# First attention layer: scores formed a second time by key tile, in place of transposed probabilities

## The chip, the cores and the metric

The kernel runs on one core of one Trainium2 chip. The metric is the device time of one execution in microseconds. The engines are TensorE (matmuls and transposes, results to PSUM), VectorE, ScalarE and GpSimd, each with a queue of its own that it works off in order; semaphores tie them together.

## The reference

The program is two layers, each an attention and a feed-forward part, with layer norms ahead. Only the first attention is touched. For x of 8 batches x 512 tokens x 256 columns, with 16 heads of 16 columns:

```python
q = _lora(x, Wq, Aq, Bq)   # and k, v: x @ W.T + a low-rank term, 16 heads of 16
s = jnp.einsum('bhqd,bhkd->bhqk', q, k) / math.sqrt(DH)
alibi = slopes[:, None, None] * (i - j)
mask = jnp.triu(jnp.full((T, T), -jnp.inf), 1)
s = s + alibi[None] + mask
p = jax.nn.softmax(s, axis=-1)
o = jnp.einsum('bhqk,bhkd->bhqd', p, v)
return o @ Wp.T
```

The layer norm of x goes in, and the result is added to x.

## The kernel before, in words

The first attention is `attention0` (L767). It goes batch by batch: batches 0, 1 and 7 are written out, batches 2 to 6 are one hardware loop (`run`, `batch`). A batch has 48 slots; each engine issues for slot k the work of its own function `slot`, so the order on each engine is fixed by hand. For k below 47 the slot of the batch before, number k + 48, follows in the same place, which is how the end of one batch lies in the start of the next.

A head has three slots, 3h, 3h+1 and 3h+2, for the groups of query tiles (0, 1), (2) and (3); a query tile i of 128 rows needs keys 0 to (i+1)*128. The order of one group is:

- Stack. q and k are held as sums of bf16 parts, 96 rows (`TERMS0`) and 6 more for the position term, together `K0` = 102. They lie by token in `q_stage` and `k_stage`; TensorE transposes a head's eight tiles into a work bank (L950, kind "stack"), and ScalarE (even heads, L1060) or VectorE (odd heads, L1135) copies it to one of two places of `stack`: query columns 0 to 511, key columns 512 to 1023. It is filled three slots ahead.
- Scores (L901), by query tile: a bf16 product over the 102 rows, and for the tile's last 128 columns the mask added by a product with the identity (L902). The result lies in one of two score banks `S`. It waits until the exponential of the group two before is done (`s_exp`).
- `row_max` on VectorE (L1117): the negative maximum of each row to `neg_max`.
- `exp` on ScalarE (L1037), with the negative maximum as bias, one instruction for each query tile, to `prob` in fp32.
- `transpose_probs` on TensorE (L915), four slots behind (`LAG_T`): the head's ten 128 x 128 tiles to the three banks `PT`, by key tile.
- One slot later (`LAG_EV`) the copies to `probT`: 512 columns by ScalarE (L1045), 512 and 256 by VectorE (L1125).
- PV (L929) for four heads at once, in three parts at slots 17, 20, 23 and so on every 12: fp32, the key tiles of `probT` against 32 columns of values, the heads side by side in the array.

Beside it run the other jobs of a batch (`work`), which share the two work banks `W` in turn; a fill waits until the bank's content of two fills before is taken (`taken`). They are the transposes of normalized x for the next batch ("xT", L959, slots 24 to 33), the q and k pieces ("piece", L965), the values (L972), the transposes of a four-head output ("oT", L980; taken by a reciprocal L1159 and a product L1163 into `y`), of `y` ("yT", L986) and the output projection ("proj", L992; taken by L1172 into x with its statistics L1175). ScalarE takes in the same slot (`LAG_WA` = 0), VectorE one slot later (`LAG_WV` = 1). VectorE's order within a slot is: row maximum, normalization, the takes, the copies to `probT`. GpSimd forms the bf16 parts of the pieces; before the first batch it writes constant columns into the stages, and TensorE's first fill waits for that (`s_const`).

Of the kernel before, what the change touches and what calls it, by code (L numbers as in the profile page):

```python
# [14 lines left out]
P = 128  # L15
# [16 lines left out]
K0 = TERMS0 + 6  # L32
# [18 lines left out]
LAGS0 = (4, 1)  # L51
# [715 lines left out]
def attention0(block, x_sb, stats, consts, w, sem, sb, banks, lags, at):  # L767
# [3 lines left out]
    LAG_T, LAG_EV = lags  # L771
# [12 lines left out]
    IN_GROUP = {i: (g, sum((j + 1) * P for j in tiles if j < i)) for g, tiles in enumerate(GROUP_TILES) for i in tiles}  # L784
    S, PT, W, ob = banks[0:2], banks[2:5], banks[5:7], banks[7]
# [8 lines left out]
    prob = [sb(f"prob0_{g}", [P, 2, n], F32) for g, n in enumerate(GROUP_COLS)]  # L794
    probT = sb("probT0", [P, 2, 4, T_AT[3]], F32)
    one = sb("one0", [P, 1], F32)
    neg_max = sb("neg_max0", [P, QT], F32)
# [9 lines left out]
    s_exp = sem("probs_ready")  # L807
    s_pt = sem("probs_transposed")
    s_pta = sem("probsT_first_taken")
    s_ptv = sem("probsT_rest_taken")  # L810
# [19 lines left out]
    s_one = sem("one_ready")  # L830
# [58 lines left out]
    def _(pe):  # L889
        work_banks = Banks()  # L890

        def scores(b, h, g):
# [3 lines left out]
            wait(pe, s_exp, G - 1)  # L896
            off = 0
            for i in GROUP_TILES[g]:
                L = (i + 1) * P
                out = S[(3 * h + g) % 2][:, off:off + L]  # L900
                pe.matmul(out, stack[0:K0, h % 2, i * P:(i + 1) * P], stack[0:K0, h % 2, T:T + L], start=True, stop=False)  # L901
                last = pe.matmul(out[:, L - P:L], ident_b[:, :], mask[:, :], start=False, stop=True)  # L902
                off += L
            last.then_inc(s_scores, 1)

        def transpose_probs(b, h, r):
            H = b * HEADS + h
            if r == 0:
                wait(pe, s_exp, 3 * (H + 1))
                wait(pe, s_pta, H)  # L910
            else:
                wait(pe, s_ptv, 2 * H - 2 + r)
# [4 lines left out]
            last.then_inc(s_pt, 1)  # L917

        def pv(b, c, part):
            Q = b * QUADS + c  # L920
            if part == 0:
                wait(pe, s_oT, Q)
                wait(pe, s_pta, 4 * (Q + 1))
            else:
                wait(pe, s_ptv, 8 * Q + 6 + part)
# [77 lines left out]
        def prologue():  # L1003
            pe.wait_ge(s_const, 1)
# [6 lines left out]
        def slot(cur, off, k, last):  # L1011
# [3 lines left out]
            if 0 <= k - LAG_T < GROUPS:  # L1015
                transpose_probs(b, (k - LAG_T) // 3, (k - LAG_T) % 3)
# [10 lines left out]
    def _(act):  # L1027
        work_banks = Banks()

        def exp(b, h, g):  # L1030
            wait(act, s_max, b * GROUPS + 3 * h + g + 1)
            if g == 0:
                wait(act, s_pt, 3 * (b * HEADS + h - 1))
            off = 0
            for i in GROUP_TILES[g]:
                L = (i + 1) * P
                last = act.activation(prob[g][:, h % 2, off:off + L], S[(3 * h + g) % 2][:, off:off + L], ACT.Exp, bias=neg_max[:, i:i + 1])  # L1037
                off += L
            last.then_inc(s_exp, 1)

        def take_probs(b, h):
            H = b * HEADS + h
            wait(act, s_pt, 3 * H + 1)
            wait(act, s_pv, b * QUADS + h // 4 - 1)
            act.activation(probT[:, (h // 4) % 2, h % 4, T_AT[0]:T_AT[1]], PT[0][:, :], ACT.Copy).then_inc(s_pta, 1)  # L1045
# [7 lines left out]
        def take(kind, b, *a):  # L1053
            bank, n = work_banks.next(kind)
            if kind == "stack":
                h, = a
                if h % 2 == 0:
                    wait(act, s_st, b * HEADS + h + 1)
                    wait(act, s_scores, 3 * (b * HEADS + h - 1))
# [32 lines left out]
        def slot(cur, off, k, last):  # L1092
# [4 lines left out]
            if k < GROUPS:  # L1097
                exp(b, k // 3, k % 3)
# [1300 lines left out]
```

## Time and profile before

| what | value |
|---|---|
| median of 3 runs | 2374.68 us (2374.14 to 2378.23) |
| profiled execution, whole | 2372.82 us |
| its span, first to last instruction | 2371.0 us |
| mean granted TensorE clock | 0.941 |
| TensorE busy | 1977.4 us (83%), 18502 matmuls |
| VectorE busy | 1754.0 us (74%) |
| ScalarE busy | 1472.8 us (62%) |
| GpSimd busy | 1034.1 us (44%) |
| first score matmul of this attention | 60.7 us |
| end of this attention | about 646 us |

A busy share is that of the whole span. The ends of matmuls are modelled, since they are pipelined; starts are recorded, so the distance from one start to the next tells what a matmul costs when TensorE does not stand.

### The profile page before, as it was taken

To read this page: it belongs to the slowest core of one execution; us is meant where nothing else is said; L and a number is where in the kernel's file an instruction comes from. 1 tells how busy PE (TensorE), PEld (TensorE's weight loads), DVE (VectorE), ACT (ScalarE), POOL (GpSimd) and SP (SyncE) were. 2 spreads that over 40 slices of the span, in tenths; PEclk is the share of its full clock that TensorE was granted. 3 is DMA by queue.
4 is the path that set the end of the run, shared out by engine and by line. 5 is a ranking of instruction groups with operands and counts; after the bars stand their busy time and mean duration, and the time that the engine had idled before them with its cause. 6 is when DMAs were issued, how large, how long until landed. Compare 5 with 4: busy or idle time off the path is not lost. (4 is left out here: it accounts for less than half of the span.)

```text
span 2371.0 us, 56863 instructions
## 1 busy us (share of the span) xinstructions
PE 1977.4 (83%) x18502; PEld 1432.5 (60%) x18503; DVE 1754.0 (74%) x3653; ACT 1472.8 (62%) x2928; POOL 1034.1 (44%) x1226
## 2 busy tenths in 40 slices
PE   2889888899862997488798999989898999639999
PEld 1667666666561665155566766666766667526665
DVE  4788878778782443477687787869697887679997
ACT  1877767677662444186678686858687787434443
POOL 4434534245014000589656465657466563042222
PEclk8999999999956999799999999999999999869999
DMA  7000000000043332002100000000000000100000
GB/s 235 2 1 2 1 1 0 1 1 1 3 144 113 100 87 74 4 13 39 15 2 3 2 3 2 2 3 2 3 2 3 2 2 2 38 0 14 18 15 25
DMA packets 53144, 57.93 MB, mean 24 GB/s; under 512 B 7120, under 2 KB 47216, under 8 KB 52896
## 3 DMA queue, kind: packets, MB, share of 16 engines
q1 hardware_dynamic: 46240, 45.00, 6.1%
q0 software_dynamic: 6656, 9.85, 2.0%
q8 instruction: 128, 2.10, 0.4%
q14 instruction: 120, 0.98, 0.1%
HBM read 36.22 MB, written 18.61 MB: 23 GB/s over the span
## 5 line engine op out<-in xcount | busy, mean ns | idle before, releaser
L1037 ACT ACTIVATE prob_sb<-a_bank,neg_max_sb 128x128 f32<-128x128 f32 (+3 forms) x512 | 258.4, 530 | 133.8 <-DVE neg_max_sb L1117 122.1
L372 PE MATMUL a_bank<-w_in_sb,xnT_sb 128*128 128x512 f16 x1152 | 289.5, 389 | 30.7 <-DVE t_buf_sb L580 22.3
L1117 DVE TENSOR_REDUCE neg_max_sb<-a_bank 128x1 f32<-128x128 f32 (+3 forms) x512 | 237.5, 485 | 101.4 <-PE a_bank L902 87.8
L532 DVE TENSOR_REDUCE neg_max_sb<-a_bank 128x1 f32<-128x128 f32 (+3 forms) x512 | 235.7, 481 | 97.3 <-PE a_bank L289 96.6
L435 ACT ACTIVATE prob_sb<-a_bank,neg_max_sb 128x128 f32<-128x128 f32 (+3 forms) x512 | 259.7, 538 | 58.6 <-DVE neg_max_sb L532 55.9
L443 ACT ACTIVATE p_hi_sb<-a_bank 128x384 f16<-128x384 f32 (+1 forms) x384 | 204.9, 534 | 112.2 <-PE a_bank L298 111.1
L539 DVE TENSOR_TENSOR p_lo_sb<-a_bank,p_hi_sb 128x384 f16<-128x384 f32 (+1 forms) x384 | 227.5, 594 | 52.3 <-ACT p_hi_sb L443 49.8
L454 ACT ACTIVATE stack_sb<-a_bank 128x1024 f16<-128x1024 f16 (+1 forms) x256 | 210.1, 821 | 32.2 <-PE a_bank L343 30.5
L298 PE MATMUL a_bank<-ident_f_sb,prob_sb 128*128 128x128 f32 x1280 | 206.9, 276 | 0.6 <-ACT prob_sb L435 0.6
L915 PE MATMUL a_bank<-ident_f_sb,prob_sb 128*128 128x128 f32 x1280 | 205.9, 276 | 0.0
L708 POOL TENSOR_TENSOR rope_w_sb<-t_buf_sb,sin_sb 128x256 f32<-128x256 f32 x128 | 125.3, 979 | 169.6 <-DVE t_buf_sb L580 167.7
L318 PE MATMUL a_bank<-v_stage_sb,p_hi_sb 128*128 128x65 f16 x1280 | 159.2, 194 | 36.7 <-DVE y_sb L551 35.9
L372 PEld LDWEIGHTS a_bank<-w_in_sb,xnT_sb 128*128 128x128 f16 x1152 | 104.5, 100 | 138.4 <-DVE t_buf_sb L580 30.7
L284 PE MATMUL a_bank<-stack_sb 128*128 128x128 f16 (+3 forms) x512 | 149.4, 304 | 39.5 <-ACT prob_sb L435 29.3
L714 POOL TENSOR_TENSOR rope_z_sb<-rope_u_sb,rope_w_sb 128x512 f32<-128x512 f32 x128 | 162.4, 1269 | 24.0 <-POOL rope_w_sb L710 21.4
L1220 POOL TENSOR_TENSOR parts_sb<-rest_sb,one_sb 128x256 bf16<-128x256 f32 x64 | 39.2, 613 | 297.7 <-DVE rest_sb L1142 296.5
L580 DVE SCALAR_TENSOR_TENSOR t_buf_sb<-a_bank,bias_sb 128x512 f32<-128x512 f32 x192 | 131.5, 685 | 43.5 <-PE a_bank L372 31.0
L319 PE MATMUL a_bank<-v_stage_sb,p_hi_sb 128*128 128x65 f16 x1280 | 160.0, 197 | 0.0
L320 PE MATMUL a_bank<-v_stage_sb,p_lo_sb 128*128 128x65 f16 x1280 | 158.2, 193 | 0.0
L285 PE MATMUL a_bank<-stack_sb 128*128 128x128 f16 (+3 forms) x512 | 155.3, 303 | 0.0
L901 PE MATMUL a_bank<-stack_sb 102*128 102x128 bf16 (+3 forms) x512 | 143.0, 305 | 12.3 <-ACT prob_sb L1037 10.3
L587 DVE TENSOR_TENSOR rope_u_sb<-t_buf_sb,cos_sb 128x512 f32<-128x512 f32 x128 | 131.4, 1027 | 28.7 <-POOL rope_z_sb L714 16.3
(259 smaller groups left out, 5503.5 us busy)
## 6 DMA issues: line engine op xcount, KB each, us to landing
sorted_rows<-zeros_sb SPq DMA_DIRECT2D x1, 4992.0 KB, 22.4
x_in_sb<-sorted_rows SPq DMA_DIRECT2D x39, 128.0 KB, 2.1
sorted_results<-y_moe_sb SPq DMA_DIRECT2D x39, 128.0 KB, 1.7
x_sb_sb<-L_attn_x SPq DMA_DIRECT2D x8, 512.0 KB, 10.5
w_raw_sb<-L_ffn_gate_bank SPq DMA_DIRECT2D x8, 512.0 KB, 3.5
w_raw_sb<-L_ffn_up_bank SPq DMA_DIRECT2D x8, 512.0 KB, 4.4
w_raw_sb<-L_ffn_down_bank SPq DMA_DIRECT2D x8, 512.0 KB, 6.0
out<-x_sb_sb SPq DMA_DIRECT2D x32, 128.0 KB, 1.7
```

The costliest lines, as they stand in the source:

```text
L298: last = pe.transpose(PT[g][:, n * P:(n + 1) * P], prob[g][:, n * P:(n + 1) * P], ident_f[:, :])
L319: pe.matmul(o, hi, v[:, 65:130], start=False, stop=False)
L372: last = pe.matmul(out, xnT[:, x, c, j * P:(j + 1) * P], w["in"][:, w_, c, cols], start=k == 0, stop=k == len(terms) - 1)
L435: last = act.activation(prob[g][:, off:off + L], S[(3 * h + g) % 2][:, off:off + L], ACT.Exp, bias=neg_max[:, i:i + 1])
L443: act.activation(p_hi[g][:, h % 2, :], PT[g][:, 0:GROUP_COLS[g]], ACT.Copy).then_inc(s_hi, 1)
L454: act.activation(dst, src, ACT.Copy).then_inc(s_stev, 1)
L532: last = dve.tensor_reduce(neg_max[:, i:i + 1], S[(3 * h + g) % 2][:, off:off + L], AX.X, ALU.max, negate=True)
L539: dve.tensor_tensor(p_lo[g][:, h % 2, :], PT[g][:, 0:GROUP_COLS[g]], p_hi[g][:, h % 2, :], ALU.subtract).then_inc(s_lo, 1)
L714: pool.tensor_tensor(rope_z[:, p % 2, :, :], rope_u[:, p % 2, :, :], rope_w[:, :, :], ALU.add).then_inc(s_z, 1)
L915: last = pe.transpose(PT[r][:, n * P:(n + 1) * P], prob[g][:, h % 2, off + kt * P:off + (kt + 1) * P], ident_f[:, :])
L1037: last = act.activation(prob[g][:, h % 2, off:off + L], S[(3 * h + g) % 2][:, off:off + L], ACT.Exp, bias=neg_max[:, i:i + 1])
L1117: last = dve.tensor_reduce(neg_max[:, i:i + 1], S[(3 * h + g) % 2][:, off:off + L], AX.X, ALU.max, negate=True)
```

## The change

The probabilities are no longer transposed. TensorE forms the scores of a head a second time, by key tile: for key tile kt the 128 keys are the stationary operand and the query columns kt*128 to 511 the moving one, so that the result has keys on partitions as PV needs it. ScalarE's exponential reads that bank and writes `probT` directly, in three instructions of 512, 512 and 256 columns, with no bias.

The row maxima are subtracted inside the second product. `K0` grows by two rows, 96 and 97: 1.0 on the key side, 0.0 on the query side, so the first scores do not feel them. VectorE splits the four negative maxima of a row into two bf16 parts (`split_max`, behind the head's third `row_max`) in columns 96 and 97 of `max_parts`; TensorE brings them to partitions 96 and 97 of bank `MT` by four bf16 products with the identity (`transpose_max`, in slot 3h+4); VectorE (even heads) or ScalarE (odd heads, ahead of its exponential) copies those two rows of 512 columns over the zeros in `stack` (`put_max`). The by-key scores (`scores_by_key`) follow in slot 3h+6. `stack` and `neg_max` have four and two places, `prob` and the three banks `PT` are gone, and two banks `ST` and one `MT` take their place. The scores by query tile now wait for the row maximum of two groups before, not for its exponential. Before the first batch GpSimd fills the new rows and the zero part of `max_parts`.

```diff
-K0 = TERMS0 + 6
+K0 = TERMS0 + 8
-LAGS0 = (4, 1)
+LAGS0 = (4, 6)
...
-    T_GROUPS = (((0, 0), (1, 0), (2, 0), (3, 0)), ((1, 1), (2, 1), (3, 1), (3, 3)), ((2, 2), (3, 2)))
+    KT_GROUPS = ((0,), (1, 3), (2,))
-    S, PT, W, ob = banks[0:2], banks[2:5], banks[5:7], banks[7]
+    S, ST, MT, W, ob = banks[0:2], banks[2:4], banks[4], banks[5:7], banks[7]
-    stack = sb("stack0", [P, 2, 2 * T], BF16)
+    stack = sb("stack0", [P, 4, 2 * T], BF16)
...
 # TensorE
-            wait(pe, s_exp, G - 1)
+            wait(pe, s_max, G - 1)
-        def transpose_probs(b, h, r):
-            ...
-            for n, (i, kt) in enumerate(T_GROUPS[r]):
-                g, off = IN_GROUP[i]
-                last = pe.transpose(PT[r][:, n * P:(n + 1) * P],
-                                    prob[g][:, h % 2, off + kt * P:off + (kt + 1) * P], ident_f[:, :])
+        def transpose_max(b, h):
+            H = b * HEADS + h
+            wait(pe, s_maxp, 2 * (H + 1))
+            wait(pe, s_rows, H)
+            for i in range(QT):
+                last = pe.matmul(MT[0:TERMS0 + 2, i * P:(i + 1) * P], max_parts[:, h % 2, i, :], ident_b[:, :],
+                                 start=True, stop=True)
+            last.then_inc(s_maxT, 1)
+
+        def scores_by_key(b, h, r):
+            G = b * GROUPS + 3 * h + r
+            if r == 0:
+                wait(pe, s_rows, b * HEADS + h + 1)
+            wait(pe, s_exp, G - 1)
+            off = 0
+            for kt in KT_GROUPS[r]:
+                out = ST[(3 * h + r) % 2][:, off:off + KT_COLS[kt]]
+                pe.matmul(out, stack[0:K0, h % 4, T + kt * P:T + (kt + 1) * P], stack[0:K0, h % 4, kt * P:T],
+                          start=True, stop=False)
+                last = pe.matmul(out[:, 0:P], mask[:, :], ident_b[:, :], start=False, stop=True)
+                off += KT_COLS[kt]
+            last.then_inc(s_scT, 1)
...
 # ScalarE
-        def exp(b, h, g):
-            ...
-                last = act.activation(prob[g][:, h % 2, off:off + L], S[(3 * h + g) % 2][:, off:off + L], ACT.Exp, bias=neg_max[:, i:i + 1])
-        def take_probs(b, h):
-            ...
+        def exp(b, h, r):
+            wait(act, s_scT, b * GROUPS + 3 * h + r + 1)
+            if r == 0:
+                wait(act, s_pv, b * QUADS + h // 4 - 1)
+            act.activation(probT[:, (h // 4) % 2, h % 4, T_AT[r]:T_AT[r + 1]],
+                           ST[(3 * h + r) % 2][:, 0:T_AT[r + 1] - T_AT[r]], ACT.Exp).then_inc(s_exp, 1)
+        def put_max(b, h):
+            wait(act, s_maxT, b * HEADS + h + 1)
+            act.activation(stack[TERMS0:TERMS0 + 2, h % 4, 0:T], MT[TERMS0:TERMS0 + 2, :], ACT.Copy).then_inc(s_rows, 1)
...
 # VectorE
+        def split_max(b, h):
+            H = b * HEADS + h
+            wait(dve, s_max, 3 * (H + 1))
+            wait(dve, s_maxT, H - 1)
+            hi_ = max_parts[:, h % 2, :, TERMS0]
+            dve.tensor_copy(hi_, neg_max[:, h % 2, :]).then_inc(s_maxp, 1)
+            wait(dve, s_maxp, 2 * H + 1)
+            dve.tensor_tensor(max_parts[:, h % 2, :, TERMS0 + 1], neg_max[:, h % 2, :], hi_, ALU.subtract).then_inc(s_maxp, 1)
+        def put_max(b, h):
+            wait(dve, s_maxT, b * HEADS + h + 1)
+            dve.tensor_copy(stack[TERMS0:TERMS0 + 2, h % 4, 0:T], MT[TERMS0:TERMS0 + 2, :]).then_inc(s_rows, 1)
...
+                if k % 3 == 2:
+                    split_max(b, k // 3)
+            h, r = divmod(k - LAG_M, 3)
+            if r == 0 and 0 <= h < HEADS and h % 2 == 0:
+                put_max(b, h)
...
 # GpSimd, before the first batch
+                for stage, table, row in ((q_stage, w["alibi_q"], 0.0), (k_stage, w["alibi_k"], 1.0)):
+                    pool.memset(stage[:, half, :, :, TERMS0:TERMS0 + 2].rearrange("p t h o -> p (t h) o"), row)
+                    last = copy(stage[:, half, :, :, TERMS0 + 2:K0], table[:, :, 8 * half:8 * half + 8, :])
+            last = pool.memset(max_parts[:, :, :, 0:TERMS0].rearrange("p r t o -> p (r t) o"), 0.0)
```

## Rows read from the trace of the kernel before

**Rows 1.** Busy time by stretch: start:end length, then PE, PEld, DVE, ACT, POOL, granted clock, DMA.

```profile
124.50:195.87 71.37, 65.09 (x676) 48.81 (x673) 59.31 (x138) 53.70 (x112) 30.69 (x64) 1.00 0.01 2
...
341.78:416.90 75.12, 66.50 (x676) 50.12 (x673) 59.63 (x138) 53.37 (x112) 30.72 (x64) 0.98 0.00 1
```

**Rows 2.** Timeline, TensorE, one head: start, duration, engine, line, operands, [idle before].

```profile
300.64 0.23 PE L901 MATMUL a_bank<-stack_sb 102*128 102x128 bf16 x1
...
300.93 0.39 PE L915 MATMUL a_bank<-ident_f_sb,prob_sb 128*128 128x128 f32 x2
...
301.16 0.39 PE L950 MATMUL a_bank<-ident_b_sb,q_stage_sb 128*102 128x128 bf16 x4
...
301.38 0.39 PE L950 MATMUL a_bank<-ident_b_sb,k_stage_sb 128*102 128x128 bf16 x4
...
301.60 0.33 PE L901 MATMUL a_bank<-stack_sb 102*128 102x384 bf16 x1
...
301.83 0.60 PE L915 MATMUL a_bank<-ident_f_sb,prob_sb 128*128 128x128 f32 x4
...
302.92 0.38 PE L901 MATMUL a_bank<-stack_sb 102*128 102x512 bf16 x1
...
303.20 0.60 PE L915 MATMUL a_bank<-ident_f_sb,prob_sb 128*128 128x128 f32 x4
```

**Rows 3.** Groups by line and form, 309 to 384 us: count, busy us, mean ns, idle before.

```profile
L915 PE MATMUL a_bank<-ident_f_sb,prob_sb 128*128 128x128 f32 x160 | 26.1, 278 | 0.0
...
L1037 ACT ACTIVATE prob_sb<-a_bank,neg_max_sb 128x512 f32<-128x512 f32 x16 | 11.2, 698 | 3.5 <-DVE neg_max_sb L1117 2.9
...
L1125 DVE COPY probT_sb<-a_bank 128x512 f32<-128x512 f32 x16 | 10.9, 681 | 0.0
...
L1045 ACT ACTIVATE probT_sb<-a_bank 128x512 f32<-128x512 f32 x16 | 9.7, 607 | 0.0
...
L1060 ACT ACTIVATE stack_sb<-a_bank 102x1024 bf16<-102x1024 bf16 x8 | 8.2, 1024 | 0.0
...
L1135 DVE COPY stack_sb<-a_bank 102x1024 bf16<-102x1024 bf16 x8 | 5.4, 681 | 0.0
```

**Rows 4.** Waits, 348 to 416 us: who waited for whom, us in total, times, longest.

```profile
PEld a_bank L986 <- DVE y_sb L1163: 1.4, 1, 1.4
...
PEld a_bank L959 <- issue: 1.4, 1, 1.4
...
PEld a_bank L965 <- ACT stack_sb L1060: 1.2, 1, 1.2
...
PEld a_bank L965 <- DVE stack_sb L1135: 1.1, 1, 1.1
...
PE a_bank L929 <- ACT v_stage_sb L1078: 0.6, 1, 0.6
```

**Rows 5.** Timeline, slots 26 and 27 of a batch, VectorE and one fill.

```profile
309.18 0.69 DVE L1117 TENSOR_REDUCE neg_max_sb<-a_bank 128x1 f32<-128x512 f32 x1 [0.54 <-PE a_bank L902]
...
309.79 0.41 DVE L1181 TENSOR_SCALAR xn_sb<-x_sb_sb,mv_sb,rstd_sb 128x256 f32 x1
...
310.11 0.42 DVE L1172 SCALAR_TENSOR_TENSOR x_sb_sb<-a_bank,x_sb_sb 128x256 f32 x1
...
310.58 0.28 PEld L950 LDWEIGHTS a_bank<-ident_b_sb,q_stage_sb 128*102 128x102 bf16 x4 [0.29 <-DVE x_sb_sb L1172]
...
311.54 0.25 DVE L1159 RECIPROCAL rsum_sb<-a_bank 128x16 f32<-128x16 f32 x1
...
311.91 0.42 DVE L1163 TENSOR_TENSOR y_sb<-a_bank,rsum_sb 128x256 f32<-128x256 f32 x1
```

**Rows 6.** Timeline, VectorE behind the edge of a loop trip.

```profile
344.81 0.62 DVE L1117 TENSOR_REDUCE neg_max_sb<-a_bank 128x1 f32<-128x128 f32 x2 [2.56 <-issue]
```

**Rows 7.** Timeline ahead of the first batch, GpSimd and TensorE.

```profile
31.08 0.50 POOL L1251 MEMSET v_stage_sb<- 128x480 f32 x1
...
33.50 0.69 PE L959 MATMUL a_bank<-ident_f_sb,xn_sb 128*128 128x128 f32 x2 [14.02 <-POOL k_stage_sb L1212]
```

More of the change, by code:

```diff
@@ L900, in scores @@
                 out = S[(3 * h + g) % 2][:, off:off + L]
-                pe.matmul(out, stack[0:K0, h % 2, i * P:(i + 1) * P], stack[0:K0, h % 2, T:T + L], start=True, stop=False)
+                pe.matmul(out, stack[0:K0, h % 4, i * P:(i + 1) * P], stack[0:K0, h % 4, T:T + L], start=True, stop=False)
                 last = pe.matmul(out[:, L - P:L], ident_b[:, :], mask[:, :], start=False, stop=True)
@@ L922, in pv @@
                 wait(pe, s_oT, Q)
-                wait(pe, s_pta, 4 * (Q + 1))
-            else:
-                wait(pe, s_ptv, 8 * Q + 6 + part)
+            wait(pe, s_exp, 12 * Q + 10 + part)
             wait(pe, s_v, b * QT + PV_KT[part][-1] + 1)
@@ L1058, in take @@
                     wait(act, s_st, b * HEADS + h + 1)
-                    wait(act, s_scores, 3 * (b * HEADS + h - 1))
-                    act.activation(stack[0:K0, 0, :], W[bank][:, :].bitcast(BF16)[0:K0, :], ACT.Copy).then_inc(s_stev[0], 1)
+                    wait(act, s_scT, 3 * (b * HEADS + h - 3))
+                    act.activation(stack[0:K0, h % 4, :], W[bank][:, :].bitcast(BF16)[0:K0, :], ACT.Copy).then_inc(s_stev[0], 1)
             elif kind == "xT":
@@ L1093, in slot @@
             b = cur + off
[L1094 to L1098 removed]
+            h, r = divmod(k - LAG_M, 3)
+            if r == 0 and 0 <= h < HEADS and h % 2:
+                put_max(b, h)
+            if 0 <= k - LAG_S < GROUPS:
+                exp(b, (k - LAG_S) // 3, (k - LAG_S) % 3)
             c, r = divmod(k - AT_OUT, 12)
@@ L1133, in take @@
                     wait(dve, s_st, b * HEADS + h + 1)
-                    wait(dve, s_scores, 3 * (b * HEADS + h - 1))
-                    dve.tensor_copy(stack[0:K0, 1, :], W[bank][:, :].bitcast(BF16)[0:K0, :]).then_inc(s_stev[1], 1)
+                    wait(dve, s_scT, 3 * (b * HEADS + h - 3))
+                    dve.tensor_copy(stack[0:K0, h % 4, :], W[bank][:, :].bitcast(BF16)[0:K0, :]).then_inc(s_stev[1], 1)
             elif kind == "piece":
@@ L1245, in prologue @@
         def prologue():
-            pool.memset(one[:, :], 1.0).then_inc(s_one, 1)
-            pool.wait_ge(s_one, 1)
+            pool.memset(one[:, :], 1.0).then_inc(s_const, 1)
+            pool.wait_ge(s_const, 1)
             for half in range(2):
@@ L1251, in prologue @@
                 pool.memset(vs[:, :, DH + 1:VW], 0.0)
-                for stage, table in ((q_stage, w["alibi_q"]), (k_stage, w["alibi_k"])):
-                    last = copy(stage[:, half, :, :, TERMS0:K0], table[:, :, 8 * half:8 * half + 8, :])
+                for stage, table, row in ((q_stage, w["alibi_q"], 0.0), (k_stage, w["alibi_k"], 1.0)):
+                    pool.memset(stage[:, half, :, :, TERMS0:TERMS0 + 2].rearrange("p t h o -> p (t h) o"), row)
+                    last = copy(stage[:, half, :, :, TERMS0 + 2:K0], table[:, :, 8 * half:8 * half + 8, :])
+            last = pool.memset(max_parts[:, :, :, 0:TERMS0].rearrange("p r t o -> p (r t) o"), 0.0)
             last.then_inc(s_const, 1)
```

57 lines of the change are left out of this document (16 added, 41 removed).

## The prediction, made before the result was known

> **What bounds the kernel now.** I read the busy shares by stage first. The change touches the first layer's attention, which runs from 60.7 us, where its first score matmul starts, to about 646 us of a 2371.0 us span; the profiled execution took 2372.82 us, and the runs shown have a median of 2374.68, so 1.9 more. All other stages are left as they are. The stage is eight batches of 48 slots, one slot for each group of scores. The table by stretch has two of the batches: 71.37 us for the second and 75.12 us for the fifth [rows 1]. In it TensorE is busy 65.1 of 71.4 us, VectorE 59.3, ScalarE 53.7, GpSimd 30.7. TensorE's ends are modelled, so I took its work from the starts of successive matmuls in the timeline [rows 2]; of a batch of 71.4 us some 61 are work that follows without a gap. TensorE is the bound, and the other 10 us are a few places where it stands.
>
> Which places these are, the list of waits says [rows 4], for one batch: 1.4 us for `y` at the fill of the transposed output, 1.4 us at the transposes of `xn`, 1.2 us where a `piece` waits until ScalarE has emptied the bank of a stack, three rows of 1.0 to 1.1 us where VectorE has to do that (L965 stands for L972 and L992), and 0.6 us where PV waits for the values. All are the ring of two work banks, or what stands ahead of a bank's emptying in another engine's queue. The chain of waits of the page ends in the last stage and says nothing here. ScalarE's own long wait for the row maxima costs TensorE nothing except at the loop's edge.
>
> **TensorE's work.** Removed are the ten fp32 transposes of a head. Four take 0.60 us, one alone 0.28 (the grouped row), so one follows another by 0.108 [rows 2, 3]: ten are 1.08 us. Added is a second set of scores of the same widths (512, 384 with 128, and 256 columns, four mask products). By starts the set of today is 300.93 - 300.64 = 0.29, 301.83 - 301.60 = 0.23 and 303.20 - 302.92 = 0.28, together 0.80 us [rows 2]. The transposes of the maxima are four ordinary bf16 products with 128 moving columns; four such follow in 301.38 - 301.16 = 0.22 [rows 2]. So 1.02 is added for 1.08: -0.06 a head, -1.0 us a batch. Bounds: if the four cost what the fp32 ones do (0.43), it is +2.4 a batch; if their loads and the masks hide wholly behind their neighbours, -0.28 a head and -4.5 a batch. I take -1.0, since shapes and types are those of the rows.
>
> **ScalarE and VectorE.** ScalarE loses a head's four exponentials and a 512-column copy of 0.61 and gets three exponentials (512, 512 and 256 columns) and every other head's copy of the two rows. A copy of 512 columns costs 0.61 on ScalarE and 0.68 on VectorE on 128 partitions, and one of 1024 columns 1.02 and 0.68 on 102 [rows 3]; I take 0.6 and 0.68 for the two rows, between 0.3 and 1.0. ScalarE is relieved by about 0.5 us a head. VectorE loses a copy of 0.68 [rows 3] and one of half its columns, and gets half a row copy (0.34) and the split. The split is two instructions on four columns with a wait for its own result before each. A reduction of 0.69 lets its neighbour start after 309.79 - 309.18 = 0.61; with a wait on it that becomes 0.75. A reciprocal on 16 columns (0.25) with such a wait behind it takes 311.91 - 311.54 = 0.37 to the next start [rows 5]. So the split makes VectorE's slot longer by 0.14 + 0.37 + 0.1 = 0.6 us; bounds 0.3 and 0.9. Neither engine bounds the batch before or after; what counts is how the standing places move.
>
> By the Trainium skill, page "VectorE: DVE Perf Modes", section on the DRAIN, a semaphore between two VectorE instructions costs nothing extra. The rows speak against it: 0.25 us of work takes 0.37 to the next start. By the page the split would be some 0.25 us cheaper, and the time about 6 us lower.
>
> **The standing places, per batch** (each is the chain of the other engine from the start of a score group, less TensorE's work in the same time):
> - `y` in slot 15: VectorE copies 512 columns of transposed probabilities ahead of it (0.68, next start after 0.60). That goes: -0.7.
> - The stack emptied by VectorE, three times: the chain (reduction 0.55, copy 0.68) stays, TensorE has 0.58 us of by-key scores and maxima transposes beside it in place of 0.44: -0.13 each, -0.4.
> - The stack emptied by ScalarE (slot 34): its exponential no longer waits for this slot's maxima but for scores issued six slots after their query-side group, so it is over while TensorE fills the stack: 1.2 becomes 0.3 to 0.4: -0.8.
> - The values (slot 23): same reason, -0.4 of 0.6.
> - Where VectorE's slot with the split stands ahead of a bank's emptying, the stall grows. The next stack fill (slot 27) waits today until VectorE has updated x: reduction at 309.18, update at 310.11, fill at 310.58 after 0.29 idle [rows 5]. The update moves back 0.6, and TensorE reaches the place 0.2 earlier (0.17 by-key work in place of 0.44, then 0.28 for 0.22): +0.8, of which the `xn` stall behind it returns 0.2. The same pattern without x, a `piece` taken behind the split, is met in slots 3, 33 and 39: chain 0.48 to the reduction's start, 0.75 and 0.45 for it and the split, 0.42 for the take and 0.06 for its signal, 2.15 us, against TensorE work of 0.28 + 0.17 + 0.44 + 0.30 + 0.28 = 1.47: +0.3, +0.2, +0.55, since a part stands already. Together +1.65.
>
> Sum of the places: -2.3 + 1.65 = -0.6 a batch. With the work -1.6, and over eight batches -13 us.
>
> **Waits that are added.** The by-key scores of a head wait for its two rows. Behind the maxima's transposes in slot 3h+4 come 0.2 us, the row copy 0.6, then in the odd heads the exponential of 0.69 on ScalarE: 1.5 us. TensorE has until slot 3h+6 a fill (0.65, from 302.92 less the end of four transposes at 302.27 [rows 2]), 0.28 + 0.17, PV or an output transpose (0.44 at least) and 0.30: 1.8 us. Hidden, with 0.3 to spare. VectorE's rows have 1.7 us in 2.4. The score banks are now free after the maximum, not after the exponential; the by-key banks two slots later after theirs: hidden, as ScalarE is idle a quarter of the time.
>
> **Edges.** At each of five loop trips VectorE starts 2.56 us late without a cause in the profile, and TensorE stands behind it nearly as long [rows 6]. It saves the exponential behind the maximum (about 0.7) but has the split ahead: -0.2 each, -1. Before the first score TensorE waits for GpSimd's preparations, the last copy having begun just before 33.50; four small memsets and one of 768 bf16 elements are added; one of 480 fp32 takes 0.50 [rows 7]: +1, bounds 0.5 and 1.5. Queues of DMA are not touched.
>
> Sum: 2372.8 - 13 - 1 + 1 = 2359.8 on the profiled execution, 2361 on the median. For the clock I take 1 us off: the batches from the fifth on show 0.98 granted against 1.00 [rows 1], half speed for about 2 us behind the loop's edge, and shorter standing there may spare some. Forecast 2360.
>
> By the Trainium skill, "TensorE: Matmul & The Clock Gate", Part 4 (PE-mode transpose), transposes don't count as activity for the clock. The second batch holds 1.00 with 160 fp32 transposes in it [rows 1], so they alone do not bring the clock down here. By the page ordinary products in their place would keep the late batches at 1.00, some 1 us each for four: 4 us less.
>
> **Rivals.**
> - The split is cheap and the freed engines show through: without the +1.65, -3.3 a batch, -26, and 2346. For it: VectorE's idle time ahead of the reduction (0.5 us in slots like that at 309.18). Against: the update stands right behind it. 0.22.
> - All cancels: the growth behind the split is as large as the rest, or TensorE's four products cost 0.1 more than by the rows: 2368 to 2379, middle 2373. 0.16.
> - Slower: the row copy stands ahead of the exponential in ScalarE's queue and waits there for TensorE, so that TensorE stands for the by-key bank in each odd head. With 1.02 for the copy and a late start the chain is 2.1 or 2.2 us against 1.8, and with a missed cover of PV (0.5) 0.8: 64 heads by 0.6 is 38 us, 2398. It decides over 0.2 us a head (13 / 64). For it: ScalarE is in order and nothing else is ahead; against: every such slot has a fill. 0.17.
> - The forecast: 0.45.
>
> **Numbers.** Differences under 0.2%, 4.7 us, cannot be told from none here. Faster by more: nearly all of the first rival and 0.42 of the forecast's 0.45, 0.63; same: 0.19; slower 0.18. Range 2334 to 2388: both unknown prices (copy 0.3 to 1.0, split 0.3 to 0.9) and part of the slower case; the forecast's own is 2345 to 2370.
>
> **What would show it.** In the profile after: 16 heads' by-key scores in starts of 0.29, 0.23 and 0.28; no L915; a batch of 69 to 71 us for the second; `y` and the ScalarE-emptied stack gone from or small in the waits; new idle time of TensorE behind `rest` and x updates; the row copy 0.6 to 0.7. Wrong would be: TensorE idle at the by-key scores with the exponential or the rows as releaser, or a split far from 0.6.

## The result, and the profile after

The changed kernel takes 2378.35 us (median of 20 runs, 2373.31 to 2385.98) against 2374.4 for the kernel before (20 runs on the same chip): a ratio of 1.0015, 95% interval 1.0008 to 1.0022. It is 4 us slower. The forecast was 2360.

The page of the kernel after, busy times; its span is 2375.7 us and the granted clock 0.934 (before: 2371.0 and 0.941):

```profile
PE 1978.2 (83%) x18758; PEld 1407.1 (59%) x18759; DVE 1745.6 (73%) x3717; ACT 1403.9 (59%) x2736; POOL 1034.4 (44%) x1231
```

Busy time by stretch after, columns as in [rows 1]: the second batch (written out), the third (the loop's first), the fifth:

```profile
125.35:195.37 70.02, 63.38 (x709) 44.95 (x704) 57.89 (x146) 44.57 (x86) 30.68 (x64) 1.00 0.01 2
195.37:267.83 72.46, 65.27 (x710) 45.76 (x704) 58.74 (x147) 44.76 (x86) 30.61 (x64) 0.98 0.01 2
342.97:417.93 74.96, 65.65 (x709) 45.63 (x704) 58.84 (x147) 44.87 (x86) 30.61 (x64) 0.98 0.00 1
```

The eight batches, from first score to first score and the last one to the end of the stage, were 63.8, 71.4, 71.7, 74.3, 75.1, 75.3, 75.1, 78.7 us and are now 63.4, 70.0, 72.5, 75.1, 75.0, 75.2, 75.0, 78.9. The written-out second batch is 1.35 us shorter. The five in the loop are 1.3 us longer together, where nine less were forecast. With 1.3 us more ahead of the first batch the stage ends 1.1 us later. The rest of the 4.7 us between the two spans arises in code that is the same in both: 3.4 us in the second attention. TensorE is at half clock there for 42.9 us in place of 36.3 us. In the kernels of this document, with one stand at each edge, a middle trip of that attention's loop without half clock took 128.6 to 128.8 us, one with 3.4 us of it 130.0 to 130.5 and one with 5.9 us 131.2 to 131.8, so most of the 3.4 us goes with the clock. What sets the clock there no run shows. Leaving aside the three written-out kernels before, its length varied from 1020.2 to 1026.8 us.

Waits after in a window of 350 to 420 us (about a batch, as [rows 4]):

```profile
PEld a_bank L901 <- DVE neg_max_sb L1122: 6.0, 10, 1.2
...
PEld a_bank L958 <- DVE rest_sb L1153: 1.8, 2, 0.9
...
PEld a_bank L958 <- DVE x_sb_sb L1183: 1.2, 1, 1.2
...
PEld a_bank L994 <- DVE y_sb L1174: 1.0, 1, 1.0
...
PEld a_bank L973 <- DVE stack_sb L1146: 0.8, 1, 0.8
```

`y` went from 1.4 to 1.0 and the piece behind ScalarE's stack is gone, as forecast. New are two fills behind `rest` and one behind the update of x. The first row is weight loads that wait while products still run; by the starts TensorE stands at a score group only at the loop's edge (slot 2). By the starts of successive matmuls, where TensorE stood in the fifth batch (all us):

| slot, what is late | before | after | change | forecast |
|---|---|---|---|---|
| 2, VectorE behind the loop's edge | 2.28 | 2.77 | +0.49 | -0.2 |
| 3, fill behind the split (second batch; in the fifth 0 and 0.83) | 0.37 | 0.83 | +0.46 | +0.3 |
| 15, `y` | 1.43 | 0.97 | -0.46 | -0.7 |
| 19, 25, 31, stack by VectorE | 2.93 | 2.55 | -0.38 | -0.4 |
| 23, values | 0.77 | 0.32 | -0.45 | -0.4 |
| 27, fill behind x | 0.21 | 1.02 | +0.81 | +0.8 |
| 27, `xn` | 1.40 | 1.40 | 0 | -0.2 |
| 29, PV at half clock | 0 | 0.40 | +0.40 | - |
| 33 and 39, fills behind the split | 0.14 | 0.90 | +0.76 | +0.75 |
| 34, piece behind ScalarE's stack | 1.08 | 0 | -1.1 | -0.8 |
| 45, fill behind the split | 0 | 0.66 | +0.66 | - |

With the smaller distances within PV, which are about the same in both, it comes to 13.87 us of standing before and 15.27 after. What is left of the batch is TensorE's work: 61.24 before, 59.69 after, 1.55 less, where 1.0 was forecast. Where a distance begins to count as standing moves these sums: with all that exceeds the usual distance of the same pair of instructions by 0.1 us, standing is 14.9 and 16.7 in the fifth batch, 11.9 and 12.2 in the second.

The fifth batch holds one thing more. Behind the two stands of slot 27 the granted clock falls to half, for 3.4 us that cover slots 28 and 29. This happens in all five batches of the changed loop, and not in the written-out second one; the kernel before has such a stretch behind the edge in three of its five (346.78, 421.87 and 496.97 us). Columns as in [rows 1], after and then before:

```profile
388.47:391.88 3.41, 3.41 (x24) 1.72 (x21) 2.49 (x6) 0.98 (x2) 0.00 (x0) 0.50 0.00 0
```

```profile
346.78:350.19 3.41, 3.41 (x24) 3.11 (x22) 2.66 (x8) 1.92 (x4) 1.52 (x3) 0.50 0.01 2
```

Slots 28 and 29 together take 4.58 us in each of the five and 2.98 in the second batch: such a stretch costs 1.60 us.

Two of the prices that the prediction had to bound, groups by form, 350 to 420 us (columns as in [rows 3]); each copy of two rows costs nearly what 128 would:

```profile
L1137 DVE CAST stack_sb<-a_bank 2x512 bf16<-2x512 f32 x8 | 5.6, 696 | 0.4 <-PE a_bank L911 0.2
...
L1050 ACT ACTIVATE stack_sb<-a_bank 2x512 bf16<-2x512 f32 x7 | 4.1, 590 | 2.2 <-PE a_bank L911 1.8
```

And slot 26 and 27 of the fifth batch, timeline, the place of [rows 5]:

```profile
383.66 0.69 DVE L1122 TENSOR_REDUCE neg_max_sb<-a_bank 128x1 f32<-128x512 f32 x1 [0.87 <-PE a_bank L902]
384.38 0.18 DVE L1131 CAST max_parts_sb<-neg_max_sb 128x4 bf16<-128x4 f32 x1
384.60 0.18 DVE L1133 TENSOR_TENSOR max_parts_sb<-neg_max_sb,max_parts_sb 128x4 bf16<-128x4 f32 x1
384.85 0.41 DVE L1192 TENSOR_SCALAR xn_sb<-x_sb_sb,mv_sb,rstd_sb 128x256 f32 x1
385.18 0.42 DVE L1183 SCALAR_TENSOR_TENSOR x_sb_sb<-a_bank,x_sb_sb 128x256 f32 x1
385.65 0.28 PEld L958 LDWEIGHTS a_bank<-ident_b_sb,q_stage_sb 128*104 128x104 bf16 x4 [1.19 <-DVE x_sb_sb L1183]
385.65 0.43 PE L958 MATMUL a_bank<-ident_b_sb,q_stage_sb 128*104 128x128 bf16 x4 [0.86 <-DVE x_sb_sb L1183]
```

Without the split the normalization would start 0.61 after the reduction, at 384.27; it starts at 384.85. The split costs 0.58, the forecast's 0.6. The fill behind it stands 0.86 by this view and 1.02 by the starts. In the written-out second batch the same place costs less: its reduction starts at 163.13, so the split takes 164.15 - 163.13 - 0.61 = 0.41 there:

```profile
163.86 0.18 DVE L1131 CAST max_parts_sb<-neg_max_sb 128x4 bf16<-128x4 f32 x1
164.07 0.18 DVE L1133 TENSOR_TENSOR max_parts_sb<-neg_max_sb,max_parts_sb 128x4 bf16<-128x4 f32 x1
164.15 0.41 DVE L1192 TENSOR_SCALAR xn_sb<-x_sb_sb,mv_sb,rstd_sb 128x256 f32<-128x256 f32 x1
```

### The profile page after: what moved, and what is told of

Read it like the earlier page. It is cut to its first block and busy times, and to the rows that moved or that the text cites. A ratio compares the mean times of both kernels' runs of the same rounds, so it can differ in the third digit from the quotient of the medians.

```text
span 2375.7 us, 57042 instructions
## 1 busy us (share of the span) xinstructions
PE 1978.2 (83%) x18758; PEld 1407.1 (59%) x18759; DVE 1745.6 (73%) x3717; ACT 1403.9 (59%) x2736; POOL 1034.4 (44%) x1231
## 5 line engine op out<-in xcount | busy, mean ns | idle before, releaser
L435 ACT ACTIVATE prob_sb<-a_bank,neg_max_sb 128x128 f32<-128x128 f32 (+3 forms) x512 | 259.7, 538 | 59.4 <-DVE neg_max_sb L532 55.2
L1045 ACT ACTIVATE probT_sb<-a_bank 128x512 f32<-128x512 f32 (+1 forms) x384 | 199.2, 526 | 149.0 <-PE a_bank L925 145.4
L298 PE MATMUL a_bank<-ident_f_sb,prob_sb 128*128 128x128 f32 x1280 | 207.4, 277 | 0.6 <-ACT prob_sb L435 0.6
L901 PE MATMUL a_bank<-stack_sb 104*128 104x128 bf16 (+3 forms) x512 | 144.1, 308 | 9.6 <-DVE neg_max_sb L1122 7.8
L298 PEld LDWEIGHTS a_bank<-ident_f_sb,prob_sb 128*128 128x128 f32 x1280 | 135.8, 142 | 26.5 <-ACT prob_sb L435 0.7
```

The source lines that it names most:

```text
L298: last = pe.transpose(PT[g][:, n * P:(n + 1) * P], prob[g][:, n * P:(n + 1) * P], ident_f[:, :])
L435: last = act.activation(prob[g][:, off:off + L], S[(3 * h + g) % 2][:, off:off + L], ACT.Exp, bias=neg_max[:, i:i + 1])
L1045: act.activation(probT[:, (h // 4) % 2, h % 4, T_AT[r]:T_AT[r + 1]], ST[(3 * h + r) % 2][:, 0:T_AT[r + 1] - T_AT[r]], ACT.Exp).then_inc(s_ ...
```

## The experiments

Each was timed against the kernel before on the same chip (2373.4 to 2375.5 there). All are edits of the changed kernel unless they say otherwise. The first four ask whether it is the split.

**Split a slot later.** `split_max` at the start of the next slot, ahead of that slot's maximum, so that no take stands behind it.

```diff
-                if k % 3 == 2:
-                    split_max(b, k // 3)
# and ahead of row_max of slot k
+            if k % 3 == 0 and 0 < k <= GROUPS:
+                split_max(b, k // 3 - 1)
```

> Edit: the split of the maxima (two VectorE instructions of 0.18 us, with a wait between) is moved from behind the head's third row maximum to the start of the next slot, behind all takes of its slot. Theory A (the split stands ahead of the emptying of work banks, and TensorE stands for those banks): in the profile after, TensorE stands 0.8 at slot 3, 1.0 at 27, 0.2 at 33, 0.7 at 39 and 0.66 at 45 of a batch at the next stack or xn fill; these fall to about 0.4, 0.2, 0, 0.1 and 0, with up to 0.3 given back at the xn transposes of slot 27: 2.2 us less a batch, 17 us in eight, so some 2361 us. Rival B (the place of the split is indifferent, since the wait for the row copy or for the by-key exponential would take its place): 2376 to 2380, with TensorE idle at L923 instead.

2364.18 us, ratio 0.9951 (0.9939 to 0.9963), 14 less than the change. The stands at 3, 39 and 45 shrink to 0.4, under 0.2 and under 0.2; new ones at 4 and 40 (0.7 each in the second batch) pay most of it back, so that the written-out second batch takes 69.66 in place of 70.02. The place of the split is worth 14 us in all: 8.7 of them in the five looped batches, 2.0 in the first batch and 1.6 behind the last score.

**No split.** The maxima are not subtracted; the exponential has a scale of 0.001 in exchange, and both parts of the maxima stay zero.

```diff
-                    split_max(b, k // 3)
-            wait(pe, s_maxp, 2 * (H + 1))
+            wait(pe, s_max, 3 * (H + 1))
```

> Edit: the two split instructions are left out altogether; the maxima part stays zero, the maxima's transposes wait for the third row maximum, and the exponential has a scale of 0.001 so that it stays finite. So the maxima are not subtracted and the scores are scaled. Theory A: as with the split moved, 2.2 us a batch, and 0.3 more where VectorE's queue is full, 2355 to 2361 us; this prices the split at all. Rival B (what costs is the row copy ahead of the exponential on ScalarE, or the longer way to the first by-key scores): under 4 us less than the changed kernel, 2375 or more. Rival C (the two short instructions are dear because they stretch beside GpSimd's work, 0.18 to 0.43 us): this kernel is over 6 us faster than the one with the split moved.

2338.91, ratio 0.9839 (0.9827 to 0.9852). This is 39 less than the change, far more than the split's standing places: the second batch took 68.0 us and the five in the loop 68.5. The 2.6 us of VectorE at each trip's edge [rows 6] were gone, though nothing had been done to the edge.

**Both lags one lower.**

```diff
-LAGS0 = (4, 6)
+LAGS0 = (3, 5)
```

> Edit: LAGS0 from (4, 6) to (3, 5): the maxima's transposes and row copy in slot 3h+3, the by-key scores five slots behind the first ones. Theory A: the end of the last batch loses a slot: in the changed kernel the last first-scores group to the end of the attention takes 3 us longer than before, TensorE idle for the by-key exponentials and then at half clock for a PV of 4.0 us; a slot less gives 1 to 3 us back. But the transposes now come one slot behind the split, and VectorE's chain of about 1.7 us against 1.6 to 1.8 of TensorE's work adds stalls of 0 to 0.2 a head, 0 to 20 us. Together 2375 to 2395. Rival B (the distance is not what the end costs): no change there, the end still 3 us longer.

2404.31, ratio 1.0119 (1.0105 to 1.0134). ScalarE waits 9.8 us a batch for the maxima's transposes ahead of its exponential, where it waited 1.8. This is the first half of the slower rival, and with the lags of the change it is hidden. The second half is not seen: TensorE hardly stands at the by-key scores (0.3 us of loads, behind VectorE's rows). It stands at the fills of the work banks, 1.1 to 1.3 us in slots 4, 15, 19, 25, 31 and 40 of the fourth batch and 2.3 in slot 27.

**The loop written out.**

```diff
-        with eng.Fori(2, B - 1) as b:
-            ...
+        for b in range(2, B - 1):
+            batch(b, False, False)
```

> Edit: the changed kernel with batches 2 to 6 written out like the others, no hardware loop in this attention. Theory A (a loop trip's first slots cost: VectorE starts 2.6 us late, TensorE then stands 2.1 + 0.7 + 0.8 us): all batches take 70.0 us as the second, which is written out, in place of 72.5, 75.1, 75.0, 75.2 and 75.0: 23 us less, about 2355 us. Rival B (later batches are slower for another reason, such as the clock or the longer program's code fetched in time for none): the batches stay at 72 to 75 us and the time above 2370.

2353.47, ratio 0.9911 (0.9894 to 0.9928). Of the six middle batches five took 70.02 and one 71.56. The two kinds side by side:

```profile
334.58:404.60 70.02, 63.38 (x708) 44.92 (x705) 58.09 (x147) 44.52 (x86) 30.68 (x64) 1.00 0.01 2
404.60:476.16 71.56, 64.99 (x709) 45.43 (x705) 58.41 (x147) 44.52 (x86) 30.68 (x64) 0.98 0.01 1
```

The second has a stretch of half clock at 446.8 to 450.2 us, in slots 28 and 29, which take 4.58 us in place of 2.98 as in the loop; the standing in slot 27 ahead of it is the same in both. So the clock alone makes 1.55 us of a batch, and here it fell in one batch of six, in the loop in all five. Against five batches of 70.02 the loop costs the changed kernel 22.7 us.

**One bf16 part.** The maxima need no second part: the sum of each row comes from the same probabilities, so a rounded maximum cancels. `row_max` writes straight into `max_parts`, and the split goes.

```diff
-                last = dve.tensor_reduce(neg_max[:, h % 2, i:i + 1], ...
+                last = dve.tensor_reduce(max_parts[:, h % 2, i, TERMS0:TERMS0 + 1], ...
-                    split_max(b, k // 3)
```

> Edit: no split. The row maximum writes its negative directly as one bf16 part into the column of max_parts (the second part stays zero); rounding it changes numerator and row sum alike, so the softmax stays the same. Everything else as in the changed kernel, nothing is left out of the computation. Theory D (the split cost 36 us in the kernel without it, 13 to 14 by its place, some 2 us a batch by VectorE's time, and five loop trips of 4 us because VectorE's loop body of about 320 queue entries lost 70 of them): 2337 to 2342 us, all batches of 68.5 us, no idle time of VectorE over 1 us at a loop trip. Rival B (the earlier gain came from exponentials of scaled scores or from the maxima not being there): 2355 or more.

2337.56, ratio 0.984 (0.9825 to 0.9854), with all of the computation. Written out and looped batch:

```profile
121.44:189.47 68.03, 63.39 (x712) 44.93 (x704) 51.58 (x114) 44.53 (x86) 30.58 (x64) 1.00 0.01 2
326.37:394.82 68.45, 63.47 (x712) 44.97 (x704) 51.66 (x115) 44.71 (x86) 30.54 (x64) 1.00 0.00 0
```

Inside a written-out batch the split cost 70.02 - 68.03 = 2.0 us. A looped one lost 74.96 - 68.45 = 6.5 with it; the other 4.5 us come only in the loop. There is no half clock in any middle batch of this kernel: TensorE's stands in slot 27 are 0.4 and 1.4 us, where they were 1.0 and 1.4.

**The kernel before, its loop written out.** The same edit as above.

> Edit: the kernel before, with batches 2 to 6 written out, no hardware loop in this attention. Theory A (the edge of a trip costs both kernels, here 2.3 us of standing and up to 1 of half clock): all batches take 71.4 us, so 71.7 - 71.4 + 2.9 + 3.7 + 3.9 + 3.7 = 14.5 us less, about 2360 us. Against it the changed kernel written out (2353) is then faster by 7 us, 8 batches of 1.35 less the start (1.3) and a longer end (1.4 and more): the change pays 7 to 9 us once the edges are gone. Rival B (the unrolled program gains elsewhere): gain here as large as the changed kernel's, 22 us or more.

2379.07, ratio 1.0015 (1.0006 to 1.0024): 2360 was expected. The batches all took 71.36, and the stage's last instruction ended 14.3 us sooner (631.4 against 645.7; the 15.6 of the expectations below is nearer to how much sooner the second attention began, 15.8). The second attention, whose code is the same, took 1041.6 us in place of 1022.2. I had no reason for that then; the last experiment gives one.

**One part, early transposes.** TensorE's wait for GpSimd's preparations moved behind the four transposes of `xn`, which don't need them.

```diff
-            pe.wait_ge(s_const, 2)
             for j in range(QT):
                 fill(0, 0, "xT", j)
+            pe.wait_ge(s_const, 2)
```

> Edit: as the kernel with one bf16 part, and TensorE waits for GpSimd's preparations behind the four transposes of normalized x ahead of the first batch, not ahead of them. Theory A (that wait costs the changed kernel 1.0 us and both kernels 1.8 more, as TensorE could start at 31.7 in place of 34.8 us): 2.5 to 3 us less than the kernel with one part. Rival: something later in the first pieces bounds, 0 to 0.5 us less.

2334.47 (2331.07 to 2337.86), ratio 0.9831 (0.9817 to 0.9845), the lowest median of all kernels here, though its interval overlaps that of the one-part kernel. The first score starts at 58.8 in place of 62.2.

**What brings the edge back.** The one-part kernel with 48 entries more in VectorE's part of a batch, each a wait that is met already. By the trace VectorE has 253 entries in a trip of the one-part kernel and 301 with these; the kernel before has 332 and the changed one 325.

```diff
             wait(dve, s_scores, G + 1)
+            if True:
+                wait(dve, s_scores, G)
```

> Edit: the kernel with one bf16 part, and behind VectorE's wait ahead of each row maximum a second, already fulfilled wait: some 100 to 140 more entries in VectorE's queue in a loop trip, no more work. Theory D (what sets VectorE's idle time at a loop trip is how many entries its loop body has): the 2.5 us of idle time and TensorE's standing behind it come back in batches 2 to 6, 4 to 6 us each, so 20 to 30 us more than with one part, beside 0 to 3 us for the waits. Rival E (it was the time of VectorE's instructions, or where the split stood at the trip's end): batches stay at 68.5 to 69, under 5 us more.

2355.06, ratio 0.9922 (0.9906 to 0.9937), 17.5 more. The written-out batch is the same to 0.01 us and the loop's first the same at 68.5; the four behind an edge take 71.9 without half clock and 73.1 to 73.2 with a stretch of it. VectorE at the edge, timeline (`neg_max` is `max_parts` here):

```profile
333.50 1.09 DVE L1124 TENSOR_REDUCE max_parts_sb<-a_bank 128x1 bf16<-128x128 f32 x3 [2.65 <-issue]
```

The DMA view tells what it waits for. Queues in the loop, 256 to 532 us of the one-part kernel and then 260 to 550 us of this one:

```profile
DMA packets 0, 0.00 MB, mean 0 GB/s; under 512 B 0, under 2 KB 0, under 8 KB 0
```

```profile
q14 instruction: 19, 0.16, 0.2%
```

No instructions are brought in during the first one's loop; in the second 19 pieces of 8 KB are, the first of a trip some 2 us before VectorE goes on. The kernel before and the changed one have the same 19 in 270 to 568 us. One falls within each idle time, as at 344 to 347 us of the changed kernel, whose VectorE stands until 346.88:

```profile
q14 instruction: 1, 0.01, 0.8%
```

Since only VectorE's program was lengthened, I take q14 for its instruction queue, and VectorE's part of the loop body to be loaded anew in each trip once it passes a size. That VectorE stands for a piece is read from these times. The prediction took this edge for a fixed cost.

**A third of them.** The 16 extra waits only behind the third group of a head.

```diff
-            if True:
+            if g == 2:
```

> As the kernel with one-part maxima (no split, 2337.6), but VectorE's queue gets 16 more entries per batch, each a wait that is already met, in place of the 48 that brought 2.65 us of idle time without a cause back at every loop trip (2355.1). Theory A, the edge appears when VectorE's part of the loop body passes a certain number of queue entries, which lies between 0 and 48 more: either no edge idle at all and 2338 +-2, or the full one and 2354 +-2, and nothing between. Rival B, the idle time grows with the number of entries: a third of it, some 0.9 us of VectorE at each edge, and 2342 to 2344. In both, the 16 waits themselves cost nothing inside a batch (68.0 us for the second).

2339.51 (2333.81 to 2343.66), ratio 0.984 (0.9818 to 0.9861). No idle time at the edge, looped batches of 68.5, no instruction piece between 256 and 532 us. It is a threshold: 16 entries more (269 in a trip) stay below, 48 (301) pass it.

**One slot less between maxima and scores.** The one-part kernel with early transposes and `LAGS0 = (4, 5)`.

```diff
-LAGS0 = (4, 6)
+LAGS0 = (4, 5)
```

> As the one-part kernel with the early transposes of xn (2334.5), but the by-key scores of a head come one slot sooner (slot 3h+5 in place of 3h+6), and what follows them too. Theory A, the row copy and ScalarE's exponential are hidden only by the two slots between: TensorE then stands at each head's by-key scores for some 0.3 to 0.6 us, as in the kernel with both lags one lower (2404.3, 29 more than before), so 2345 to 2365. Rival B, that kernel's loss came from the maxima's transposes in slot 3h+3, which wait for the split in the same slot, and not from the scores: then the cover of one slot is enough, and the last batch's end gets a slot shorter, some 1.5 us: 2333.

2351.75, ratio 0.9902 (0.9885 to 0.9918), 17 more than with six. TensorE stands for 0.22 to 0.76 us at the by-key scores of seven of the eight even heads, whose rows VectorE copies:

```profile
PEld a_bank L923 <- DVE stack_sb L1137: 2.6, 7, 0.4
```

So the row copies are hidden with two slots between the maxima's transposes and the by-key scores and not with one. What shows is VectorE's copy in the even heads, not ScalarE's in the odd ones that the slower rival named.

**The kernel before, written out, early transposes.** Does its loss in the second attention hang on when the engines get there?

```diff
-            pe.wait_ge(s_const, 1)
             for j in range(QT):
                 fill(0, 0, "xT", j)
+            pe.wait_ge(s_const, 1)
```

> The kernel before with the five loop batches of the first attention written out, and with TensorE's wait for GpSimd's preparations behind the four transposes of xn. The same without the second edit took 2379.1: 15.6 us less in the first attention, 19.4 more in the untouched second one. Theory A, that loss in the second attention belongs to the written-out form (its code lies elsewhere, or the engines reach it in another order) and comes again: first score some 3 us sooner, second attention 1041 +-2, total 2374 to 2378. Rival B, it hangs on the relative times with which the engines reach the second attention, and a start that differs by 3 us changes it: second attention 1020 to 1026 and total 2355 to 2360.

2376.59, ratio 1.0006 (0.9996 to 1.0016), second attention 1039.7. It does not. The timeline of the one without the early transposes (TensorE, first trip's edge of the second attention) shows the loss: two stands without a cause, 3.2 us apart, where the kernel before has one of 2.4 to 2.9 us per trip. Without and with the early transposes there are ten such stands at the five edges, in the kernel before five.

```profile
1269.37 0.23 PE L284 MATMUL a_bank<-stack_sb 128*128 128x128 f16 x1 [2.81 <-issue]
...
1272.56 0.40 PE L284 MATMUL a_bank<-stack_sb 128*128 128x256 f16 x1 [2.85 <-issue]
```

**Its code moved by 40 entries.** The written-out kernel before, and in TensorE's program, once, behind the first attention:

```diff
         run(pe, prologue, slot, [work_banks.t], next_batch)
+        for _ in range(40):
+            pe.wait_ge(s_const, 1)
```

> The kernel before with the first attention's loop batches written out (2379.1: first attention 15.6 us shorter, the untouched second one 19.4 longer, since TensorE stands twice for 2.8 us at each of its five loop trips where it stood once), and 40 waits that are already met put into TensorE's program once, behind the first attention. They do nothing but move all its later code by 40 entries. Theory A, the second stand at each trip comes from where the loop's code lies against the 16 KB pieces in which the instruction queue brings it: with the code moved, TensorE stands once per trip again, the second attention takes 1021 to 1026 us and the whole 2359 to 2365. Rival B, the second stand comes from the first attention being written out as such (more code in all, other arrival of the engines): nothing changes, second attention 1040 to 1042, the whole 2377 to 2380. Should the move put another boundary in a bad place, a number of stands other than two per trip would show it, which speaks for A as well.

2363.19 (2361.25 to 2367.11), ratio 0.9945 (0.9925 to 0.9965), 16 less than without the 40 waits. One stand at each of the five edges again, the second attention 1027.4:

```profile
1272.85 0.28 PE L284 MATMUL a_bank<-stack_sb 128*128 128x128 f16 x1 [2.81 <-issue]
```

Entries that do nothing made the written-out kernel before faster by 16 us. The early transposes changed when the second attention is reached and did not help; the 40 waits moved its code and did. That leaves the place of the code as the cause, seen from its effect.

## Why the prediction was wrong

The steps inside a batch were mostly right; what failed is the edge of the loop and the clock, put at -1 each. Together they were to give 2 us back and cost 8.0 more. From first to last instruction the forecast's own sum, with the clock, comes to 14 us less, and 4.7 more were measured. Of these 19 us, 11.3 lie in the five looped batches (-10 forecast, +1.3 measured), 3.4 in the second attention, 1.9 in the last batch, 1.2 in the first, 0.4 ahead of it and 0.3 in the second. By its steps:

- **The edges, -0.2 each, and the clock, -1: the step that failed.** The written-out kernels separate the loop from the batch itself: 71.36 before and 70.02 after, so the change gains 1.34 a batch where there is no loop, near the forecast's 1.6. The loop cost 371.5 - 5 x 71.36 = 14.7 us before and costs 372.8 - 350.1 = 22.7 after, five batches each. These 8 us eat the gain of the five. 5.4 of them are the clock: stretches of half clock cost 5 x 1.60 + 0.2 = 8.2 us in the changed loop, and the three in the kernel before 2.8 (its fifth to seventh batches, slots 0 to 4, against the fourth, which has none). The forecast had expected shorter standing at the edge to spare some of the clock; instead it fell at a new place, behind the longer standing that the split makes in slot 27. The rest is standing. VectorE's idle time is the same (2.57 after, 2.56 before), but the stack's copy and the output's transposes now wait behind it with the split (2.77 us at slot 2, where 2.28 were), and in slot 27 the loop adds 0.48 us a batch, where it added 0.27. Part of this can be seen: in the loop the normalization starts 0.25 us behind the split's second instruction (384.85 - 384.60), in the written-out second batch 0.08. That the entries around a short instruction are no longer hidden in the loop is an inference. The loop's first trip has no idle time at its edge and takes 72.46 against 70.02: 1.6 of these 2.4 us are the clock, 0.5 slot 27, 0.4 slots 3 and 4.
- **Standing places, -0.6 a batch: wrong in sign.** Ten of the twelve listed came within 0.25 of their forecast, `y` (0.46 of 0.7) and `xn` (nothing) on the dear side; the edge did not. Missed altogether was slot 45, a fill like those at 3 and 39 (+0.66; 0.41 without the split, as TensorE has less beside it there). Slot 29 is the clock. Standing grew by 0.3 to 0.6 us in the second batch and by 1.4 to 1.8 in the fifth, by where one draws the line. The split's own price of 0.6 was right in the loop and is 0.41 outside; it has to be met in every slot that holds one, and I had not gone through all of them.
- **TensorE's work, -1.0 a batch.** Measured at -1.55 in the fifth batch and between -1.6 and -1.9 in the second. Better than forecast by 0.6 to 0.9, and this made up for the standing where there is no loop: that the written-out batch came so near is partly luck.
- **First and last batch, -1.6 each.** Measured -0.45 and +0.27. The by-key work lags by six slots, so it runs on behind the last score: from there to the end 18.3 us against 15.2. In this execution the last PV also ran at half clock:

```profile
634.20:638.30 4.10, 4.07 (x34) 1.23 (x32) 0.00 (x0) 0.55 (x2) 0.00 (x0) 0.58 0.00 0
```

  Other kernels with the same lag had about 16.6, which is some 1.4 more than the kernel before. But the kernel before with its loop written out had 15.2, 16.5 and 16.5 in three versions, so how much of the 1.4 is the lag stays open.
- **Preparations, +1.** TensorE's first transpose came 1.4 us later, of which 0.3 arose before; right.
- **The clock's rows.** The granted clock did not rise: 0.98 in the fifth batch as before, and 0.98 in the third, where the kernel before had 1.00. The stretch at half clock that the forecast took for about 2 us is 3.4 long, and in the kernel before it is in three batches, not in four. By the Trainium skill, "TensorE: Matmul & The Clock Gate", Part 4 (PE-mode transpose), a transpose doesn't count as busy time for the clock in the way a product does. If so, ordinary products in the place of fp32 transposes should have helped it; here it stood lower in the third batch without them.
- **The unknown prices.** Row copies 0.59 and 0.70 (forecast 0.6 and 0.68), exponential without bias 0.60 in place of 0.70, four products for the maxima as 0.22. The 0.37 us from the start of a reciprocal to what waits for it was read in a looped batch [rows 5]; in the written-out second batch of the same kernel it is 0.28 (165.73 to 166.01), so a wait between two VectorE instructions costs hardly anything there, and the prediction was too quick to say that the rows speak against it.

Of the rivals, "all cancels" (2368 to 2379) is the time that came. Its mechanism, growth behind the split as large as the rest, holds only with the loop: outside it the batch still gained 1.35 us. The cheap split (2346) did not come; its price was the forecast's. The split gone gives 2338, which is 41 less: by the 48 entries 17.5 us of that are the edge, some 16 are 2.0 us in each of eight batches, and the rest is not separated. The row copy ahead of the exponential costs nothing at the distance of the change; with less distance the time is higher (2351.75 and 2404.31), but TensorE then stands at other places than that rival said.

## What to carry to other kernels

A small operation in an engine's fixed order costs what stands behind it: go through every slot that holds it, not the ones that look busy. Idle time at a loop's edge that the profile gives no cause for is worth a look at the instruction queue in the DMA view: if pieces come in at each trip, a shorter body on that engine can remove the whole of it, and moving code can double it elsewhere. Look at the granted clock batch by batch as well: two stands of 1.0 and 1.4 us close together were followed by half clock in every looped batch here, at 1.6 us each. Judge such a kernel written out and looped, or the loop's cost is taken for the change's.

## What the runs showed that I had not expected

VectorE's loop body stays loaded with 16 entries more than the one-part kernel's and doesn't with 48 more; the step is worth 4 us a trip. TensorE stands some 2.8 us at an edge of the second attention once or twice, and 40 inert entries decided which. Pieces of 16 KB on another instruction queue, q8, go with it: in the written-out kernel before two begin at 1266.2 and 1269.8 us and the stands end at 1269.4 and 1272.6, in the moved one a piece begins at 1269.9 and the one stand ends at 1272.9. That TensorE waits for these pieces is read from the times. A stretch of 3.4 us at half clock cost 1.60 us, and two batches alike in all else differed by it. What sets the threshold of the loop body, where the pieces lie, and why the clock fell in one written-out batch of six and in all looped ones, no run here shows.
